# Slot products of a two-layer graph kernel: three buffers of high and low parts, and the next slot's parts ahead of the finished slot's copy

## The chip, the cores and the metric

The kernel runs on one core of a Trainium2 chip. A core has five engines that run side by side and meet only at semaphores: TensorE (PE, matrix products; its weight loads are listed apart as PEld), VectorE (DVE), ScalarE (ACT), GpSimd (POOL) and SyncE (SP, which here issues the DMA transfers). The metric is the device time of one execution in microseconds (us); lower is better.

## The reference, cut to what matters

There are 128 graphs of 128 nodes with 256 features each. Layer 0 is a gated graph convolution with a residual and a layer norm. Layer 1 convolves along the nodes, adds a similarity branch, and mixes both in a gated recurrent cell. The part of interest is the second convolution of layer 1, with 17 taps:

```python
h = _bn(_conv1d(xc, conv1_w, 0), bn1_g, bn1_b, bn1_m, bn1_v)
h = jax.nn.relu(h)
h = _bn(_conv1d(h, conv2_w, 8), bn2_g, bn2_b, bn2_m, bn2_v)
x_conv = jnp.transpose(jax.nn.relu(h + xc), (0, 2, 1))
```

## The kernel before

The kernel is four phases, each ended by a barrier. `phase_a` computes layer 0 and the spectra of the convolution filters (`w_spec` in device memory). `phase_spectrum` computes conv1 and the spectra of its result, which stay on chip in `x_spec`. `phase_product` multiplies the spectra; it is the only phase whose instructions the change alters. `phase_c` transforms back and does the rest of layer 1.

The 17-tap convolution is done as a product of spectra of length 136. Two real rows, a real and an imaginary one, make a slot, so there are 68 slots (`SLOTS`). For a slot s the following is done, once each:

- SP loads the slot's filters, 512 KB, into one of 4 buffers `w` (line 718).
- ACT makes the high part `xh` of the slot's data (line 754) and the high part `wh` of its filters (line 757). DVE makes the low parts by subtraction, `xl` (line 774) and `wl` (line 785).
- PE does 18 matmuls of three passes (low by high, high by low, high by high): 6 with 512 columns and 12 with 256, into one of 4 buffers of `ps` (line 799).
- ACT copies the sums from `ps` to `y` (line 750), and DVE subtracts the product of the imaginary parts (line 781, below called the subtraction).
- SP stores `y`, 256 KB, to `y_spec` (line 729). The first four slots, the rest slots (`REST`), are instead split into `yh` (ACT, line 763) and `yl` (DVE, line 789), and both are stored to `y_rest` (line 726).

Every engine runs the helper `pipeline` over the same step number i. Step i is: SP loads slot i and then stores slot i-3; ACT copies slot i-3 and then makes `xh` and `wh` of slot i-1; DVE makes `xl` of slot i-1, subtracts slot i-3, and makes `wl` of slot i-1; PE multiplies slot i-2. Each engine does its instructions strictly in this order, and each waits for semaphores that count finished slots. The waits that matter here:

- the load of slot i waits until `wl` of slot i-4 is made;
- the store of slot s waits for the subtraction of slot s;
- `xh`, and so `wh` behind it, of slot s waits until PE has finished slot s-2, since there are two buffers of the parts;
- `wh` also waits until its filters have landed; the copy waits until PE has finished its slot;
- the matmuls wait for `xl` and `wl`.

The first 12 steps are written out, the others run in a loop whose body holds 4 steps. Both kernels have this wait of the load and this order on SP:

```python
if live(0):
    reached(sp, s_wl, i - BUFS + 1)
    sp.dma_start(w[:, u]...)
if live(3):
    ...
        reached(sp, s_ys, s)
        sp.dma_start(y_spec[...], y[:, b])
```

Of the kernel before, what the change touches and what calls it, by code (L numbers as in the profile page):

```python
# [7 lines left out]
F32 = mybir.dt.float32  # L8
F32R = mybir.dt.float32r
ALU = mybir.AluOpType  # L10
ACT = mybir.ActivationFunctionType

P = 128
D = 256
KD = D // P
# [7 lines left out]
SLOTS = L // 2  # L23
# [3 lines left out]
CW = 64  # L27
# [3 lines left out]
def reached(eng, sem, count):  # L31

    if isinstance(count, int) and count <= 0:
        return
    eng.wait_ge(sem, count)


def pipeline(eng, units, stages, step, peeled=0, unroll=2):


    first = max(stages, peeled)
    first += -first % unroll
    for i in range(first):
        step(i, i % unroll, i // unroll, lambda s, i=i: 0 <= i - s < units)
    with eng.Fori(first // unroll, units // unroll) as block:
        for u in range(unroll):
            step(block * unroll + u, u, block, lambda s: True)
    for i in range(units, units + stages - 1):
        step(i, i % unroll, i // unroll, lambda s, i=i: 0 <= i - s < units)


# [617 lines left out]
def phase_product(nc, G, x_spec, w_spec, y_spec, y_rest):  # L669


    BUFS = 4
    with ExitStack() as ctx:  # L673
        def sb(name, shape, dt=F32):
            return ctx.enter_context(nc.sbuf_tensor("m_" + name, shape, dt))
# [3 lines left out]


        w = sb("w", [P, BUFS, KD, CHUNKS, 2, CW])
        wh = sb("wh", [P, 2, KD, CHUNKS, 2, CW], F32R)
        wl = sb("wl", [P, 2, KD, CHUNKS, 2, CW], F32R)
        xh = sb("xh", [P, 2, KD, 2, G], F32R)
        xl = sb("xl", [P, 2, KD, 2, G], F32R)
        y = sb("y", [P, BUFS, 2, D])
        yh = sb("yh", [P, 2, 2, D], F32R)
        yl = sb("yl", [P, 2, 2, D], F32R)
# [16 lines left out]
        block = ctx.enter_context(nc.Block())  # L705

        STAGES = 4
        assert SLOTS % BUFS == 0 and REST == BUFS

        def is_rest(s):  # L710
            return isinstance(s, int) and s < REST
# [1 line left out]
        @block.sync  # L713
        def _(sp):
            def step(i, u, k, live):
                if live(0):
                    reached(sp, s_wl, i - BUFS + 1)
                    sp.dma_start(w[:, u].rearrange("p t q r c -> p (t q) (r c)"),
                                 w_spec.rearrange("n p d c -> p n d c")[:, :, bass.ds(2 * i, 2)].rearrange("p n d c -> p n (d c)")
                                 ).then_inc(s_w[u], 16)  # L720
                if live(3):
                    s, b = i - 3, (u - 3) % BUFS
                    if is_rest(s):
                        reached(sp, s_yl, s + 1)
                        for part, rows in enumerate((yh, yl)):
                            sp.dma_start(y_rest[part, 2 * s:2 * s + 2].rearrange("d g c -> g d c"), rows[:, s % 2].bitcast(F32)).then_inc(s_rest[s % 2], 16)
                    else:
                        reached(sp, s_ys, s)
                        sp.dma_start(y_spec[bass.ds(2 * s - 2 * REST, 2)].rearrange("d g c -> g d c"), y[:, b]).then_inc(s_out[b], 16)

            pipeline(sp, SLOTS, STAGES, step, peeled=3 * BUFS, unroll=BUFS)
            for u in range(BUFS):
                sp.wait_ge(s_out[u], 16 * (SLOTS // BUFS - 1))
            for u in range(2):
                sp.wait_ge(s_rest[u], 16 * REST)

        @block.scalar
        def _(act):
            def step(i, u, k, live):
                if live(3):  # L740
                    s, b = i - 3, (u - 3) % BUFS
                    reached(act, s_m, s + 1)
                    if isinstance(s, int) and REST <= s < 2 * REST:

                        act.wait_ge(s_yl, s - REST + 1)
                    if not is_rest(s):

                        at_block = k if b <= u else k - 1
                        reached(act, s_out[b], (at_block - 1) * 16)
                    nc.scalar.activation(y[:, b], ps[:, b, 0], ACT.Copy).then_inc(s_yc, 1)  # L750
                if live(1):
                    s, b, v = i - 1, (u - 1) % BUFS, (u - 1) % 2
                    reached(act, s_m, s - 1)
                    nc.scalar.activation(xh[:, v], x_spec[:, :, bass.ds(s, 1)].rearrange("p c o r g -> p c (o r) g"), ACT.Copy).then_inc(s_xh, 1)
                    at_block = k if b <= u else k - 1
                    reached(act, s_w[b], (at_block + 1) * 16)
                    nc.scalar.activation(wh[:, v], w[:, b], ACT.Copy).then_inc(s_wh, 1)
                if live(3) and is_rest(i - 3):
                    s, b = i - 3, (u - 3) % BUFS
                    reached(act, s_yc, s + 1)  # L760
                    reached(act, s_ys, s)
                    reached(act, s_rest[s % 2], 32 * (s // 2))
                    nc.scalar.activation(yh[:, s % 2], y[:, b], ACT.Copy).then_inc(s_yh, 1)

            pipeline(act, SLOTS, STAGES, step, peeled=3 * BUFS, unroll=BUFS)

        @block.vector
        def _(dve):
            def step(i, u, k, live):
                if live(1):  # L770
                    s, b, v = i - 1, (u - 1) % BUFS, (u - 1) % 2
                    reached(dve, s_xh, s + 1)
                    reached(dve, s_m, s - 1)
                    nc.vector.tensor_tensor(xl[:, v], x_spec[:, :, bass.ds(s, 1)].rearrange("p c o r g -> p c (o r) g"),
                                            xh[:, v].bitcast(F32), ALU.subtract).then_inc(s_xl, 1)
                if live(3):
                    s, b = i - 3, (u - 3) % BUFS

                    if not (isinstance(s, int) and s == 0):
                        reached(dve, s_yc, s + 1)  # L780
                        nc.vector.tensor_tensor(y[:, b, 0], y[:, b, 0], ps[:, b, 1, 0], ALU.subtract).then_inc(s_ys, 1)
                if live(1):
                    s, b, v = i - 1, (u - 1) % BUFS, (u - 1) % 2
                    reached(dve, s_wh, s + 1)
                    nc.vector.tensor_tensor(wl[:, v], w[:, b], wh[:, v].bitcast(F32), ALU.subtract).then_inc(s_wl, 1)
                if live(3) and is_rest(i - 3):
                    s, b = i - 3, (u - 3) % BUFS
                    reached(dve, s_yh, s + 1)
                    nc.vector.tensor_tensor(yl[:, s % 2], y[:, b], yh[:, s % 2].bitcast(F32), ALU.subtract).then_inc(s_yl, 1)

            pipeline(dve, SLOTS, STAGES, step, peeled=3 * BUFS, unroll=BUFS)

        @block.tensor
        def _(pe):
            def three_passes(out, part, v, filters, start, stop):

                for c in range(KD):
                    for t, (xx, ww) in enumerate(((xl, wh), (xh, wl), (xh, wh))):
                        last = nc.tensor.matmul(out.rearrange("p r (q c) -> p r q c", q=CHUNKS), xx[:, v, c, part],  # L799
                                                ww[:, v, c].rearrange("p q r c -> p r q c")[:, filters],  # L800
                                                start=start and c == 0 and t == 0, stop=stop and c == KD - 1 and t == 2)
                return last

            def step(i, u, k, live):
                if live(2):
                    s, b, v = i - 2, (u - 2) % BUFS, u % 2
                    reached(pe, s_xl, s + 1)
                    reached(pe, s_wl, s + 1)
                    reached(pe, s_ys, s - BUFS)
                    reached(pe, s_yc, s - BUFS + 1)  # L810
                    re, im, both = slice(0, 1), slice(1, 2), slice(0, 2)
                    if isinstance(s, int) and s == 0:
                        three_passes(ps[:, b, 0, re], 0, v, re, True, True)
                        three_passes(ps[:, b, 0, im], 1, v, im, True, True).then_inc(s_m, 1)
                    else:
                        three_passes(ps[:, b, 0], 0, v, both, True, False)
                        three_passes(ps[:, b, 0, im], 1, v, re, False, True)
                        three_passes(ps[:, b, 1, re], 1, v, im, True, True).then_inc(s_m, 1)

            pipeline(pe, SLOTS, STAGES, step, peeled=3 * BUFS, unroll=BUFS)  # L820


def phase_c(nc, G, x1_t, y_spec, y_rest, dft_i, bn2, masks, adj_t, w_ih, w_hh, w_msg, w_se, b_ih, b_hh, b_msg, b_se, form, y_n):
# [739 lines left out]
```

## Time and profile before

| | |
|---|---|
| median of 3 runs | 2383.63 us (2381.34 to 2383.7) |
| the profiled execution's own time | 2387.73 us |
| its span, first to last instruction | 2385.9 us |
| mean granted clock of TensorE | 0.949 of full speed |
| busy over the whole span: PE, DVE, ACT, POOL | 88%, 59%, 49%, 30% |
| the product phase | from about 907 to 1151 us, a tenth of the span |

The engines' busy shares are means over four phases that have different limits. What the change is worth must be read inside the product phase, from instructions in order of time.

### The profile page before, as it was taken

The page shows a single profiled execution, that of the slowest core. Times are in us where ns is not written, and L with a number is a line of the kernel's source. Part 1 is how long each engine was busy: PE and PEld are TensorE (multiplying, and loading weights), DVE is VectorE, ACT ScalarE, POOL GpSimd, SP SyncE. Part 2 cuts the span into 40 slices and gives each one's busy share as a digit, 9 for nine tenths or more (in the row PEclk, how much of TensorE's full clock was granted, in tenths as well). Part 3 has the DMA queues.
Part 4 walks back from the last instruction along what each step waited for, and adds up shares of the span by engine and source line. Part 5 has one row for each costly group of instructions (what it writes and reads, how often), then busy time and mean ns, then how long its engine had stood idle before and what let it go on. Part 6 is the DMA issues. An engine that isn't in the chain of part 4 may idle for free.

```text
span 2385.9 us, 37395 instructions
## 1 busy us (share of the span) xinstructions
PE 2090.2 (88%) x12034; PEld 1789.0 (75%) x12034; DVE 1407.4 (59%) x2577; ACT 1180.6 (49%) x1950; POOL 706.5 (30%) x561
## 2 busy tenths in 40 slices
PE   6888788787088886888599999999999999999998
PEld 5777666676078886777478888888888888888886
DVE  5788787798033334666455655656555556565563
ACT  5677666676045555565334444444444444443442
POOL 5667666575600000000012222222222222222222
PEclk9999999898599998999699999999999999999999
DMA  3555455554122215777511211212212122121200
GB/s 119 190 205 199 138 196 201 194 199 172 50 71 70 70 53 172 228 229 230 172 66 51 83 59 65 74 50 82 72 52 82 41 82 74 50 82 50 87 29 27
DMA packets 195906, 263.57 MB, mean 110 GB/s; under 512 B 11914, under 2 KB 141680, under 8 KB 194672
## 3 DMA queue, kind: packets, MB, share of 16 engines
q1 hardware_dynamic: 195824, 262.66, 33.7%
q8 instruction: 29, 0.48, 0.1%
q14 instruction: 53, 0.43, 0.1%
HBM read 174.53 MB, written 88.08 MB: 110 GB/s over the span
## 4 chain that ended last, share of the span: by engine, by line
PE 49%; issue 1%; ACT 1%; DMA 1%; DVE 0%; SPq 0%; POOL 0%; POOLq 0%; ACTq 0%; DVEq 0%
PE c_ps_g L1353 34%; PE c_ps_s L1380 5%; PE c_ps_m L1353 4%; PE c_ps_s L1353 2%; PE c_ps_s L1424 1%; PE c_ps_y L1403 1%; PE c_ps_y L1440 1%; PE c_ps_m L1440 1%; DMA c_yf<-y_spec 1%; PE c_ps_m L1441 0%; PE c_ps_y L1441 0%; ACT c_wi_h L1114 0%; SPq L1005 0%; DVE c_t L1222 0%; SPq L1013 0%
## 5 line engine op out<-in xcount | busy, mean ns | idle before, releaser
L1176 POOL TENSOR_TENSOR c_cl<-c_xc,c_ch 128x512 fp32r<-128x512 f32 x64 | 82.6, 1291 | 488.6 <-ACT c_ch L1068 471.1
L799 PE MATMUL m_ps<-m_wh,m_xl 128*128 128x256 f32 (+1 forms) x406 | 136.9, 337 | 36.8 <-issue 17.2
L1353 PE MATMUL c_ps_g<-c_xh,c_wh_l 128*128 128x512 f32 x384 | 155.6, 405 | 4.2 <-POOL c_cl L1176 4.2
L1252 DVE TENSOR_SCALAR c_work<-c_work 128x512 f32<-128x512 f32 x64 | 27.4, 428 | 219.4 <-ACT c_work L1063 219.4
L1353 PE MATMUL c_ps_g<-c_ch,c_wi_l 128*128 128x512 f32 x384 | 153.6, 400 | 0.0
L1353 PE MATMUL c_ps_g<-c_xl,c_wh_h 128*128 128x512 f32 x384 | 152.4, 397 | 0.0
L1353 PE MATMUL c_ps_g<-c_xh,c_wh_h 128*128 128x512 f32 x384 | 151.9, 396 | 0.0
L1353 PE MATMUL c_ps_g<-c_nh,c_wi_l 128*128 128x512 f32 x384 | 151.7, 395 | 0.0
L1353 PE MATMUL c_ps_g<-c_ch,c_wi_h 128*128 128x512 f32 x384 | 151.7, 395 | 0.0
L1353 PE MATMUL c_ps_g<-c_nh,c_wi_h 128*128 128x512 f32 x384 | 151.7, 395 | 0.0
L1353 PE MATMUL c_ps_g<-c_nl,c_wi_h 128*128 128x512 f32 x384 | 151.6, 395 | 0.0
L1353 PE MATMUL c_ps_g<-c_cl,c_wi_h 128*128 128x512 f32 x384 | 151.5, 394 | 0.0
L1143 POOL MEMSET c_ident<- 128x128 f32 x1 | 0.2, 206 | 502.1 <-POOLq L673 502.1
L1156 POOL TENSOR_TENSOR c_work<-c_xg,c_work 128x512 f32<-128x512 f32 x64 | 89.4, 1397 | 182.9 <-ACT c_work L1058 160.0
L626 DVE SCALAR_TENSOR_TENSOR s_hl<-s_ps_c,s_hh 128x1024 fp32r<-128x1024 f32 x32 | 39.2, 1225 | 165.4 <-ACT s_hh L584 165.4
L799 PE MATMUL m_ps<-m_wl,m_xh 128*128 128x256 f32 (+1 forms) x406 | 130.7, 322 | 0.0
L1068 ACT ACTIVATE c_ch<-c_t,c_shift 128x512 fp32r<-128x512 f32 x64 | 46.3, 724 | 170.0 <-DVE c_t L1222 170.0
L799 PE MATMUL m_ps<-m_wh,m_xh 128*128 128x256 f32 (+1 forms) x406 | 130.3, 321 | 0.0
L799 PEld LDWEIGHTS m_ps<-m_wh,m_xl 128*128 128x128 f32 x406 | 77.9, 192 | 54.3 <-issue 36.2
L432 PE MATMUL a_ps_w<-a_dw,a_gs 102*128 102x272 f32 x256 | 80.2, 313 | 42.2 <-ACT a_spec L242 42.0
L320 POOL TENSOR_TENSOR a_res<-a_ex,a_xn 128x512 f32<-128x512 f32 x64 | 105.8, 1653 | 20.0 <-DMA a_xn<-in_x_n 16.1
L1165 POOL TENSOR_TENSOR c_rstd<-c_var_eps,c_neg_half 128x4 f32<-128x4 f32 x32 | 32.6, 1019 | 265.7 <-DVE c_var_eps L1285 265.7
(220 smaller groups left out, 7300.2 us busy)
## 6 DMA issues: line engine op xcount, KB each, us to landing
w_spec<-a_spec SPq DMA_DIRECT2D x8, 4352.0 KB, 16.8
m_w<-w_spec SPq DMA_DIRECT2D x68, 512.0 KB, 4.0
a_xt<-in_x_t SPq DMA_DIRECT2D x64, 256.0 KB, 3.1
a_xn<-in_x_n SPq DMA_DIRECT2D x64, 256.0 KB, 6.6
x_t<-a_x1t SPq DMA_DIRECT2D x64, 256.0 KB, 2.9
s_x<-x_t SPq DMA_DIRECT2D x32, 512.0 KB, 3.9
y_spec<-m_y SPq DMA_DIRECT2D x64, 256.0 KB, 2.4
c_x<-x_t SPq DMA_DIRECT2D x32, 512.0 KB, 4.1
```

The source lines that it names most:

```text
L320: nc.gpsimd.tensor_tensor(res[:, u], ex[:, :, :], xn[:, u], ALU.add).then_inc(s_res, 1)
L432: nc.tensor.matmul(ps_w[:, 0:GW], gs[:, u, c], dw[:, :], start=True, stop=True).then_inc(s_gm, 1)
L626: nc.vector.scalar_tensor_tensor(hl[:, u], ps_c[:, u], 0.0, hh[:, u].bitcast(F32), ALU.max, ALU.subtract).then_inc(s_hl, 1)
L799: last = nc.tensor.matmul(out.rearrange("p r (q c) -> p r q c", q=CHUNKS), xx[:, v, c, part], ww[:, v, c].rearrange("p q r c -> p r q c")[ ...
L1068: nc.scalar.activation(ch[:, v, j], t2[:, j], ACT.Relu, bias=shift2[:, j:j + 1]).then_inc(s_ch, 1)
L1156: nc.gpsimd.tensor_tensor(dd[:, :], xg[:, v, j], nn[:, :], ALU.subtract).then_inc(s_dd, 1)
L1165: nc.gpsimd.tensor_tensor(rstd[:, :], var_eps[:, :], neg_half[:, :], ALU.pow).then_inc(s_rstd, 1)
L1176: nc.gpsimd.tensor_tensor(cl[:, v, j], xc[:, j], ch[:, v, j].bitcast(F32), ALU.subtract).then_inc(s_cl, 1)
L1252: nc.vector.tensor_scalar(zz[:, :], tz[:, :], 0.5, 0.5, ALU.mult, ALU.add).then_inc(s_zz, 1)
L1353: last = nc.tensor.matmul(out, stationary, moving, start=(n == 0), stop=(n == len(passes) - 1))
L1380: last = nc.tensor.matmul(ps_s[:, b * P:b * P + P], stationary, moving, start=(n == 0), stop=(n == len(passes) - 1))
L1440: nc.tensor.matmul(both, mh[:, b, j * P:j * P + P], ahl[:, b].rearrange("p s n -> p (s n)"), start=True, stop=False)
```

## The change

The parts `wh`, `wl`, `xh`, `xl` get three buffers (`SPLIT`) in place of two, so `xh` of slot s waits for PE to finish slot s-3. On ACT, `xh` and `wh` of slot i-1 now come ahead of the copy of slot i-3. On DVE, `xl` and `wl` of slot i-1 both come ahead of the subtraction of slot i-3. The order on SP and the order on PE stay. The loop body now holds 12 steps, the first 12 steps are written out as before, and the last 11 are written out as well (3 before). The line in `pipeline` changes nothing where the units are a multiple of the unroll, as in the other phases.

```diff
-    for i in range(units, units + stages - 1):
+    for i in range(units - units % unroll, units + stages - 1):
...
+    SPLIT = 3
...
-        wh = sb("wh", [P, 2, KD, CHUNKS, 2, CW], F32R)
-        wl = sb("wl", [P, 2, KD, CHUNKS, 2, CW], F32R)
-        xh = sb("xh", [P, 2, KD, 2, G], F32R)
-        xl = sb("xl", [P, 2, KD, 2, G], F32R)
+        wh = sb("wh", [P, SPLIT, KD, CHUNKS, 2, CW], F32R)
+        wl = sb("wl", [P, SPLIT, KD, CHUNKS, 2, CW], F32R)
+        xh = sb("xh", [P, SPLIT, KD, 2, G], F32R)
+        xl = sb("xl", [P, SPLIT, KD, 2, G], F32R)
...
+        UNROLL = BUFS * SPLIT
+        assert REST == BUFS
+
+        def turns(k, u, back):
+
+            return k * SPLIT + (u - back) // BUFS
...
             def step(i, u, k, live):
+                if live(1):
+                    s, b, v = i - 1, (u - 1) % BUFS, (u - 1) % SPLIT
+                    reached(act, s_m, s - SPLIT + 1)
+                    nc.scalar.activation(xh[:, v], x_spec[:, :, bass.ds(s, 1)].rearrange("p c o r g -> p c (o r) g"), ACT.Copy).then_inc(s_xh, 1)
+                    reached(act, s_w[b], (turns(k, u, 1) + 1) * 16)
+                    nc.scalar.activation(wh[:, v], w[:, b], ACT.Copy).then_inc(s_wh, 1)
                 if live(3):
                     s, b = i - 3, (u - 3) % BUFS
                     reached(act, s_m, s + 1)
...
                     nc.scalar.activation(y[:, b], ps[:, b, 0], ACT.Copy).then_inc(s_yc, 1)
-                if live(1):
-                    s, b, v = i - 1, (u - 1) % BUFS, (u - 1) % 2
-                    reached(act, s_m, s - 1)
-                    nc.scalar.activation(xh[:, v], x_spec[:, :, bass.ds(s, 1)].rearrange("p c o r g -> p c (o r) g"), ACT.Copy).then_inc(s_xh, 1)
-                    at_block = k if b <= u else k - 1
-                    reached(act, s_w[b], (at_block + 1) * 16)
-                    nc.scalar.activation(wh[:, v], w[:, b], ACT.Copy).then_inc(s_wh, 1)
...
                 if live(1):
-                    s, b, v = i - 1, (u - 1) % BUFS, (u - 1) % 2
+                    s, b, v = i - 1, (u - 1) % BUFS, (u - 1) % SPLIT
                     reached(dve, s_xh, s + 1)
-                    reached(dve, s_m, s - 1)
+                    reached(dve, s_m, s - SPLIT + 1)
                     nc.vector.tensor_tensor(xl[:, v], x_spec[:, :, bass.ds(s, 1)].rearrange("p c o r g -> p c (o r) g"),
                                             xh[:, v].bitcast(F32), ALU.subtract).then_inc(s_xl, 1)
+                    reached(dve, s_wh, s + 1)
+                    nc.vector.tensor_tensor(wl[:, v], w[:, b], wh[:, v].bitcast(F32), ALU.subtract).then_inc(s_wl, 1)
                 if live(3):
                     s, b = i - 3, (u - 3) % BUFS
 
                     if not (isinstance(s, int) and s == 0):
                         reached(dve, s_yc, s + 1)
                         nc.vector.tensor_tensor(y[:, b, 0], y[:, b, 0], ps[:, b, 1, 0], ALU.subtract).then_inc(s_ys, 1)
-                if live(1):
-                    s, b, v = i - 1, (u - 1) % BUFS, (u - 1) % 2
-                    reached(dve, s_wh, s + 1)
-                    nc.vector.tensor_tensor(wl[:, v], w[:, b], wh[:, v].bitcast(F32), ALU.subtract).then_inc(s_wl, 1)
...
-            pipeline(dve, SLOTS, STAGES, step, peeled=3 * BUFS, unroll=BUFS)
+            pipeline(dve, SLOTS, STAGES, step, unroll=UNROLL)
...
-                    s, b, v = i - 2, (u - 2) % BUFS, u % 2
+                    s, b, v = i - 2, (u - 2) % BUFS, (u - 2) % SPLIT
```

## Rows read from the trace of the kernel before

**Rows 1.** Waits, product phase (us in total, times, longest); the last from SP's queue.

```profile
ACT m_y L750 <- PE m_ps L799: 89.0, 65, 3.6
...
ACT m_wh L757 <- DMA m_w<-w_spec: 11.0, 8, 3.5
...
SPq L729 <- DVE m_y L781: 140.7, 63, 4.9
```

**Rows 2.** Timeline of ACT: start us, duration us, instruction [idle before].

```profile
1040.98 0.60 ACT L750 ACTIVATE m_y<-m_ps 128x512 f32<-128x512 f32 x1 [1.66 <-PE m_ps L799]
1041.47 0.62 ACT L754 ACTIVATE m_xh<-x_spec 128x512 fp32r x1
1041.99 1.05 ACT L757 ACTIVATE m_wh<-m_w 128x1024 fp32r<-128x1024 f32 x1
...
1047.78 0.60 ACT L750 ACTIVATE m_y<-m_ps 128x512 f32<-128x512 f32 x1 [1.65 <-PE m_ps L799]
```

**Rows 3.** Timeline of DVE, the same steps.

```profile
1042.24 0.69 DVE L774 TENSOR_TENSOR m_xl<-x_spec,m_xh 128x512 fp32r<-128x512 f32 x1 [1.57 <-ACT m_xh L754]
1042.85 0.41 DVE L781 TENSOR_TENSOR m_y<-m_y,m_ps 128x256 f32<-128x256 f32 x1
1043.18 1.22 DVE L785 TENSOR_TENSOR m_wl<-m_w,m_wh 128x1024 fp32r<-128x1024 f32 x1
```

**Rows 4.** Timeline of PE: first matmul of a slot behind a stall, and of two in a row.

```profile
941.01 0.77 PE L799 MATMUL m_ps<-m_wh,m_xl 128*128 128x512 f32 x1 [2.52 <-issue]
...
1044.59 0.49 PE L799 MATMUL m_ps<-m_wh,m_xl 128*128 128x512 f32 x1 [0.65 <-issue]
...
1047.81 0.49 PE L799 MATMUL m_ps<-m_wh,m_xl 128*128 128x512 f32 x1 [0.15 <-issue]
```

**Rows 5.** SP's queue: loads of slots 12 and 67; between, two stores and loads.

```profile
951.22 0.40 SPq L718 DMA_DIRECT2D m_w<-w_spec  x1
...
1043.44 0.38 SPq L729 DMA_DIRECT2D y_spec<-m_y  x1
1044.02 0.39 SPq L718 DMA_DIRECT2D m_w<-w_spec  x1
1046.52 0.38 SPq L729 DMA_DIRECT2D y_spec<-m_y  x1
1047.43 0.39 SPq L718 DMA_DIRECT2D m_w<-w_spec  x1
...
1139.49 0.39 SPq L718 DMA_DIRECT2D m_w<-w_spec  x1
```

**Rows 6.** Landing times of the 68 filter loads and 8 stores of filters.

```profile
DMA to landing us min/median/max: 3.8/4.0/17.6
```

**Rows 7.** Timeline of ACT, DVE and SP's queue while the rest slots are stored.

```profile
924.87 1.06 ACT L757 ACTIVATE m_wh<-m_w 128x1024 fp32r<-128x1024 f32 x1 [1.37 <-DMA m_w<-w_spec]
...
925.96 1.23 DVE L785 TENSOR_TENSOR m_wl<-m_w,m_wh 128x1024 fp32r<-128x1024 f32 x1 [1.40 <-ACT m_wh L757]
...
927.11 0.69 DVE L789 TENSOR_TENSOR m_yl<-m_y,m_yh 128x512 fp32r<-128x512 f32 x1
...
927.82 0.37 SPq L726 DMA_DIRECT2D y_rest<-m_yh  x1
...
928.75 0.50 SPq L718 DMA_DIRECT2D m_w<-w_spec  x1
...
933.02 1.06 ACT L757 ACTIVATE m_wh<-m_w 128x1024 fp32r<-128x1024 f32 x1 [1.52 <-DMA m_w<-w_spec]
```

**Rows 8.** Timeline, the one place in the loop where filters were late.

```profile
967.18 1.06 ACT L757 ACTIVATE m_wh<-m_w 128x1024 fp32r<-128x1024 f32 x1 [0.32 <-DMA m_w<-w_spec]
...
968.28 1.23 DVE L785 TENSOR_TENSOR m_wl<-m_w,m_wh 128x1024 fp32r<-128x1024 f32 x1
```

**Rows 9.** Stretches: length, busy PE, PEld, DVE, ACT, POOL, clock, DMA share, GB/s.

```profile
942.00:944.00 2.00, 2.00 (x7) 1.63 (x6) 1.13 (x1) 0.00 (x0) 0.00 (x0) 0.50 0.55 162
954.00:1142.00 188.00, 167.56 (x991) 143.80 (x990) 119.33 (x168) 113.87 (x166) 0.00 (x0) 1.00 0.79 230
```

More of the change, by code:

```diff
@@ L707, in phase_product @@
         STAGES = 4
-        assert SLOTS % BUFS == 0 and REST == BUFS
+        UNROLL = BUFS * SPLIT
+        assert REST == BUFS
+        def turns(k, u, back):
+            return k * SPLIT + (u - back) // BUFS
         def is_rest(s):
@@ L717, in step @@
                     reached(sp, s_wl, i - BUFS + 1)
-                    sp.dma_start(w[:, u].rearrange("p t q r c -> p (t q) (r c)"),
+                    sp.dma_start(w[:, u % BUFS].rearrange("p t q r c -> p (t q) (r c)"),
                                  w_spec.rearrange("n p d c -> p n d c")[:, :, bass.ds(2 * i, 2)].rearrange("p n d c -> p n (d c)")
-                                 ).then_inc(s_w[u], 16)
+                                 ).then_inc(s_w[u % BUFS], 16)
                 if live(3):
@@ L729, in step @@
                         sp.dma_start(y_spec[bass.ds(2 * s - 2 * REST, 2)].rearrange("d g c -> g d c"), y[:, b]).then_inc(s_out[b], 16)
-            pipeline(sp, SLOTS, STAGES, step, peeled=3 * BUFS, unroll=BUFS)
+            pipeline(sp, SLOTS, STAGES, step, unroll=UNROLL)
             for u in range(BUFS):
@@ L746, in step @@
                     if not is_rest(s):
-                        at_block = k if b <= u else k - 1
-                        reached(act, s_out[b], (at_block - 1) * 16)
+                        reached(act, s_out[b], (turns(k, u, 3) - 1) * 16)
                     nc.scalar.activation(y[:, b], ps[:, b, 0], ACT.Copy).then_inc(s_yc, 1)
-                if live(1):
-                    s, b, v = i - 1, (u - 1) % BUFS, (u - 1) % 2
-                    reached(act, s_m, s - 1)
-                    nc.scalar.activation(xh[:, v], x_spec[:, :, bass.ds(s, 1)].rearrange("p c o r g -> p c (o r) g"), ACT.Copy).then_inc(s_xh, 1)
-                    at_block = k if b <= u else k - 1
-                    reached(act, s_w[b], (at_block + 1) * 16)
-                    nc.scalar.activation(wh[:, v], w[:, b], ACT.Copy).then_inc(s_wh, 1)
                 if live(3) and is_rest(i - 3):
@@ L763, in step @@
                     nc.scalar.activation(yh[:, s % 2], y[:, b], ACT.Copy).then_inc(s_yh, 1)
-            pipeline(act, SLOTS, STAGES, step, peeled=3 * BUFS, unroll=BUFS)
+            pipeline(act, SLOTS, STAGES, step, unroll=UNROLL)
         @block.vector
@@ L818, in step @@
                         three_passes(ps[:, b, 1, re], 1, v, im, True, True).then_inc(s_m, 1)
-            pipeline(pe, SLOTS, STAGES, step, peeled=3 * BUFS, unroll=BUFS)
+            pipeline(pe, SLOTS, STAGES, step, unroll=UNROLL)
 def phase_c(nc, G, x1_t, y_spec, y_rest, dft_i, bn2, masks, adj_t, w_ih, w_hh, w_msg, w_se, b_ih, b_hh, b_msg, b_se, form, y_n):
```

## The prediction

> **What bounds the phase now.** The change touches only the product phase, so the whole-kernel shares decide nothing, and three of the four phases keep their instructions. I read four views of the phase: the waits, the timeline of each engine around 1040 us, SP's queue, and the stretches.
>
> The waits say that ACT stood 89.0 us for PE before its copies, and only 11.0 us for filters, 8 times; and that SP stood 140.7 us for the subtraction before its stores [rows 1]. The first names today's limit. The last looks harmless, yet SP issues in order and the next load stands behind that store.
>
> Pace: the loop issues the loads of slots 12 to 67 from 951.22 to 1139.49 us, 55 intervals in 188.27 us, so 3.423 us a slot [rows 5]. PE alone would be faster: between two first matmuls lie 3.22 us with 0.15 us of idle, so some 3.07 us of work [rows 4]. What holds it at 3.42 is a circle over two slots. PE finishes slot 35 and ACT starts its copy (1040.98), then `xh` of slot 37 (+0.49), then `wh` (+0.52); DVE starts `wl` 1.19 us later, behind its subtraction; `wl` takes 1.22; PE starts slot 37 0.19 us after (1044.59) and ACT copies it at 1047.78, 3.19 us on. Sum: 0.49+0.52+1.19+1.22+0.19+3.19 = 6.80 us for two slots, 3.40 each [rows 2, 3, 4], which is the pace. (Slot numbers: load 12 is at 951.22, so the one at 1044.02 is number 39, the store before it 35.)
>
> **What the change removes.** With three buffers `xh` and `wh` of slot 37 need PE's slot 34, not 35, and stand ahead of the copy of slot 35. The circle above is cut; if nothing else held it, PE's 3.07 us would be the pace.
>
> **What the change closes.** Three orders stay or are new: the load of slot n+2 is issued behind the store of slot n-2 (SP, as before); that store waits for the subtraction of slot n-2; and this subtraction now stands behind `wl` of slot n on DVE, and its copy behind `wh` of slot n on ACT. But `wh` of slot n needs the load of slot n. So load n leads to `wh` n, `wl` n, subtraction n-2, store n-2, load n+2: a circle over two slots with a whole DMA transfer in it. Before, subtraction n-2 stood ahead of `wl` n and the copy ahead of `wh` n, so the same walk went through `wh` of slot n-1 and spanned three slots: with the numbers below, 3.95 landing, 0.97 to 0.99 `wh`, 0.49 copy, 0.77 `xh` to `xl` start, 0.61 to the subtraction's start [rows 2, 3], 0.41, 0.18, 0.65 = about 8.0 us for three, 2.7 each. Filters were on time, by 0.8 us: slot 39's load went out at 1044.02 and landed near 1048.0, its `wh` came 1.01 us behind the copy of 1047.78, at 1048.79 [rows 2, 5].
>
> The length of the new circle, term by term:
>
> - `wh` on ACT 1.05 us [rows 2], and 0.04 us to the start of `wl` where DVE waits for it: 967.18+1.06 = 968.24, `wl` at 968.28 [rows 8].
> - `wl`: the next DVE instruction starts 1.15 us behind its start (925.96 to 927.11) [rows 7], the pipelined form of its 1.22. I take 1.14. By then the copy, begun about 0.97 us after `wh`'s start, is over, so it adds nothing.
> - The subtraction 0.41; then 0.18 us to the store's issue: 1042.85+0.41 = 1043.26, issue at 1043.44 [rows 3, 5].
> - Store to load on SP: 0.58 and 0.91 us in two cases [rows 5]. The larger is the one of four steps that takes in the loop's turn; with 12 steps in the body it comes once in 12. I take 0.65.
> - Load issue to landing: median 4.0, least 3.8 [rows 6]; where ACT waited for it, `wh` started 933.02-928.75 = 4.27 us after issue in the written-out part [rows 7], whose issue itself is 0.1 us longer. I take 3.95, by the loop's median.
>
> Sum: 1.05+0.04+1.14+0.41+0.18+0.65+3.95 = 7.42 us for two slots, 3.71 a slot. That is longer than PE's 3.07 and than today's 3.42.
>
> The trace holds a test of this walk. While the rest slots are stored, `yl` stands behind `wl` in just that way: `wh` 924.87, `wl` 925.96, `yl` 927.11 (0.69), store 927.82, load 928.75, next-but-one `wh` 933.02. The whole turn is 8.15 us, and it waited for the DMA at both ends [rows 7]. The new circle has 0.41 for 0.69 and one store for two. So every link has been seen; new is that it runs for the whole loop.
>
> **The sum.** 55 intervals by (3.71-3.42) = +15.8 us. After the last load the path was: landing, 0.8 us of waiting for the copy, `wh`, `wl`, PE, copy, subtraction, store. The waiting goes, the rest is equal: -0.8 us. The written-out start: `wh` of slot 2 no longer waits for PE's slot 0, which brings the first stores up to 2 us forward; but in the four rest slots subtraction, `yh` and `yl` now all stand behind `wl`: `yh` (0.6 us) and the subtraction (0.41) join the 8.15 us turn, about +0.5 us a slot, +2 us. I take zero and keep 2 us either way. The added 8 written-out steps at the end change a link by 0.2 us or so and go into the range. Memory for the third buffers costs no time; the instructions are as many as before. PE's 0.3 to 0.4 us saved a slot lie beside the circle and are worth nothing.
>
> Total +15.0 us: 2387.73 becomes about 2402.7 for a profiled execution, which was 4.1 us above the median of the runs; on the median, 2383.63+15.0 = 2398.6 us, +0.63%. Bounds of the circle: landing 3.8 and 0.58 between store and load give 7.20 (3.60 a slot, +9.7-0.8 = +9); landing 4.27 and the mean of today's two issue gaps, 0.75, give 7.84 (3.92, +27.3-0.8 = +26.5). With the start's 2 us: 2391 to 2412.
>
> **Rivals.**
>
> 1. Faster, because loads return sooner than I think. The circle without its landing is 3.47 us; it equals today's two slots (6.85) at a landing of 3.38 us, and leaves the lead to PE (6.14) at 2.67. With PE leading, 55 by -0.35 = -19.4, and -0.8: about 2363; a landing half way gives 2373. For it: the engines of the DMA are 0.79 busy in the loop [rows 9], and slower steps would leave them emptier. Against it: the shortest landing of all is 3.8 us [rows 6]. Chance 0.10. The Trainium skill, "DMA: Bandwidth & Descriptors", section "Anatomy of one DMA", fits a transfer as 2.0 us plus bytes over 436 GB/s, for a path issued by GpSimd; by it 512 KB would land in an estimated 3.2 us, the circle would be 3.34 a slot, and the kernel would come out at 2378 us. The trace disagrees, with 3.8 us as its least, for SP's queue.
> 2. No change that can be told (within 0.2%, a bound of about what a measurement of this kernel can tell): the links in the loop overlap more than I add up, the circle is 6.7 to 7.0 us, +-4 us in all. For it: each of seven links could be 0.1 us short. Against it: the turn of 8.15 us shows nearly the same links at full length, one behind the other. Chance 0.08.
> 3. Slower by more: transfers of odd and even slots drift together and delay one another, so landings go from 4 to 4.5 us or more: 8.0 a turn, +32 us, 2415. For it: a DMA share of 0.79. Against it: store and load of a circle keep their distance, and the longer step lowers the share to about 0.73. Chance 0.06.
> 4. PE's clock. PE gets idle gaps of 0.6 us a slot on average and unequal ones may reach 1.5. Behind a stall of 2.52 us [rows 4] the clock was at the lower of its levels, 0.50 (1.2 GHz), at 942 to 944 us [rows 9]; in the loop it stands at 1.00. A single fall is hidden, since a slot's copy is needed more than 2 us after PE ends it. If it stayed low, a slot would take about 6.1 us on PE: +140 us. Chance 0.03, with the loop's longer code among what could disturb it.
>
> **Numbers.** Forecast 0.73; rivals 0.10, 0.08, 0.06, 0.03. The likeliest gives 2398.6 us. The range 2386 to 2418 reaches into rival 2 below and takes in rival 3; it leaves out rival 1, rival 4 and half of rival 2. Faster by over 0.2%: 0.10. Within: 0.08. Slower by over 0.2% (above 2388.4): 0.82.
>
> **What will show it.** In the changed kernel, nearly every `wh` of the loop should be preceded by idle time that a DMA of filters ended (some 60 times, of 0.8 us or more each, for 11.0 us before), the waits for PE before the copies should be gone from ACT, `wl` should start 0.04 us behind `wh`, the subtraction should start 1.14 us behind `wl`, and every second `wh` start should be 7.2 to 7.8 us apart. PE should wait for `wl`, and DMA share should fall to about 0.73. The prediction is wrong if landings come in well below 3.8 us, if SP's loads aren't held by the subtraction, or if the phase's own start or end moves by more than 3 us.

## The result, and the profile after

The changed kernel takes 2396.1 us (median of 4 runs, 2393.52 to 2398.76) against 2383.66 us before; the ratio is 1.0054, with a 95% interval of 1.0036 to 1.0071. It is slower by 12.4 us. The forecast was slower by 15.0, at 2398.6 us.

First the waits of the product phase after the change (who waited for whom: us in total, times, longest).

```profile
ACT m_wh L752 <- DMA m_w<-w_spec: 104.2, 65, 3.3
DVE m_wl L782 <- ACT m_wh L752: 99.3, 66, 3.6
...
ACT m_y L762 <- PE m_ps L802: 4.6, 3, 3.5
```

ACT's wait for PE before its copies has gone from 89.0 us to 4.6, as the change says it should. In its place ACT waits for filters 65 times in 68 slots, 104.2 us against 11.0 [rows 1], and DVE's `wl` waits for that `wh`. SP's own queue waits for the subtraction even longer than before, 161.6 us:

```profile
SPq L736 <- DVE m_y L788: 161.6, 63, 4.0
```

Next the timeline of ACT (start us, duration us), one turn of the circle and the `wh` in between.

```profile
1040.07 1.06 ACT L752 ACTIVATE m_wh<-m_w 128x1024 fp32r<-128x1024 f32 x1 [1.70 <-DMA m_w<-w_spec]
1041.03 0.58 ACT L762 ACTIVATE m_y<-m_ps 128x512 f32<-128x512 f32 x1
...
1043.52 1.06 ACT L752 ACTIVATE m_wh<-m_w 128x1024 fp32r<-128x1024 f32 x1 [1.39 <-DMA m_w<-w_spec]
...
1047.35 1.06 ACT L752 ACTIVATE m_wh<-m_w 128x1024 fp32r<-128x1024 f32 x1 [1.76 <-DMA m_w<-w_spec]
```

DVE in the same turn:

```profile
1041.16 1.23 DVE L782 TENSOR_TENSOR m_wl<-m_w,m_wh 128x1024 fp32r<-128x1024 f32 x1 [1.61 <-ACT m_wh L752]
1042.30 0.41 DVE L788 TENSOR_TENSOR m_y<-m_y,m_ps 128x256 f32<-128x256 f32 x1
```

and SP's queue in the same turn:

```profile
1042.89 0.38 SPq L736 DMA_DIRECT2D y_spec<-m_y  x1
1043.47 0.39 SPq L725 DMA_DIRECT2D m_w<-w_spec  x1
```

Read together, these are the predicted links in the predicted order: `wh` at 1040.07, ending 1041.13; `wl` 0.03 us later; the subtraction 1.14 us behind `wl`'s start; 0.18 us from its end (1042.71) to the store's issue; 0.58 us to the load's issue; 3.88 us to the next-but-one `wh` at 1047.35. The sum is 1.06+0.03+1.14+0.41+0.18+0.58+3.88 = 7.28 us. Over the stretch 960 to 1090 us two slots take 7.35 us on average. The early turns are the longer ones: 7.46 us on average over slots 12 to 28, 7.26 from there to slot 67.

PE waits before each slot (first matmuls of two slots in a row), where before it had stood 0.65 and 0.15 us [rows 4]:

```profile
1042.58 0.49 PE L802 MATMUL m_ps<-m_wh,m_xl 128*128 128x512 f32 x1 [0.69 <-issue]
1045.94 0.47 PE L802 MATMUL m_ps<-m_wh,m_xl 128*128 128x512 f32 x1 [0.30 <-issue]
```

SP's queue again, the loads of slots 12 and 67, and the stretch of the loop (length, busy PE, PEld, DVE, ACT, POOL, clock, DMA share, GB/s):

```profile
943.65 0.40 SPq L725 DMA_DIRECT2D m_w<-w_spec  x1
...
1144.82 0.47 SPq L725 DMA_DIRECT2D m_w<-w_spec  x1
```

```profile
954.00:1142.00 188.00, 157.35 (x926) 134.95 (x927) 110.98 (x155) 105.47 (x154) 0.00 (x0) 1.00 0.73 215
```

55 intervals in 201.17 us are 3.658 us a slot, against 3.423 [rows 5]: 55 by 0.235 = +12.9 us. The DMA share fell from 0.79 [rows 9] to 0.73, as forecast, and the clock stayed at 1.00. The whole phase, from the first filter load to the end of the last store's issue, took 256.1 us against 244.6, +11.5. The two profiled spans differ by 6.2 us only (2392.1 and 2385.9), mostly because the phases ahead of the product, which have the same instructions in both, ended 6.7 us earlier in this execution: the first filter load was issued at 899.9 us here and at 906.5 before, and between 898 and 908 us in all the profiles below. So the pace of the phase is read inside it, and whole times are compared over several runs.

### The profile page after: what moved, and what is told of

It is laid out like the page before. It is cut to its first block, busy times and chain, and to the rows that moved or that the text cites. A ratio compares the mean times of both kernels' runs of the same rounds, so it can differ in the third digit from the quotient of the medians.

```text
span 2392.1 us, 37206 instructions
## 1 busy us (share of the span) xinstructions
PE 2083.9 (87%) x12034; PEld 1783.3 (75%) x12034; DVE 1407.0 (59%) x2577; ACT 1180.2 (49%) x1950; POOL 706.4 (30%) x561
## 4 chain that ended last, share of the span: by engine, by line
PE 49%; issue 1%; ACT 1%; DMA 0%; DVE 0%; SPq 0%; POOL 0%; POOLq 0%; ACTq 0%; DVEq 0%
PE c_ps_g L1356 34%; PE c_ps_s L1383 5%; PE c_ps_m L1356 4%; PE c_ps_s L1356 2%; PE c_ps_s L1427 1%; PE c_ps_y L1406 1%; PE c_ps_y L1443 1%; PE c_ps_m L1443 1%; DMA c_yf<-y_spec 0%; PE c_ps_m L1444 0%; PE c_ps_y L1444 0%; ACT c_wi_h L1117 0%; SPq L1008 0%; SPq L1016 0%; DVE c_t L1225 0%
## 5 line engine op out<-in xcount | busy, mean ns | idle before, releaser
L782 DVE TENSOR_TENSOR m_wl<-m_w,m_wh 128x1024 fp32r<-128x1024 f32 x68 | 83.3, 1225 | 99.4 <-ACT m_wh L752 99.3
L752 ACT ACTIVATE m_wh<-m_w 128x1024 fp32r<-128x1024 f32 x68 | 72.1, 1060 | 104.3 <-DMA m_w<-w_spec 104.2
```

## The experiments

Each run was timed in turn with the kernel before on the same chip, and its ratio is to those times. "Pace" is the time a slot takes in the loop, from the loads of slots 12 and 67, or, where marked *, from the copies between 1000 and 1080 us.

| run | edit | time, us | ratio to before (95%) | pace, us |
|---|---|---|---|---|
| before | | 2381.4 to 2384.1 (medians) | | 3.423 |
| changed | | 2396.1 | 1.0054 (1.0036 to 1.0071) | 3.658 |
| E1 | changed, stores a step later | 2343.33 | 0.9822 (0.9806 to 0.9839) | 2.854 |
| E2 | changed, DVE's old order | 2385.76 | 1.0001 (0.9989 to 1.0014) | 3.408 |
| E3 | changed, both old orders | 2380.05 | 0.9988 (0.9973 to 1.0003) | 3.360 |
| E4 | changed, two buffers | 2401.17 | 1.0066 (1.0049 to 1.0082) | 3.730 |
| E5 | before, stores a step later | 2376.69 | 0.9981 (0.9970 to 0.9993) | 3.418 |
| E6 | changed, half loads | 2369.43 | 0.9954 (0.9938 to 0.9970) | 3.229 |
| E7 | changed, stores on GpSimd's queue | 2339.77 | 0.9833 (0.9802 to 0.9864) | 2.82* |
| E8 | E4, stores a step later | 2362.6 | 0.9917 (0.9893 to 0.9941) | 3.101 |
| E9 | E3, stores a step later | 2371.51 | 0.9955 (0.9942 to 0.9968) | 3.322 |
| E10 | before, DVE's new order | 2406.43 | 1.0088 (1.0064 to 1.0113) | 3.767 |

### E1: the load freed from the store

```diff
-                if live(3):
-                    s, b = i - 3, (u - 3) % BUFS
+                if live(4):
+                    s, b = i - 4, (u - 4) % BUFS
...
-            pipeline(sp, SLOTS, STAGES, step, unroll=UNROLL)
+            pipeline(sp, SLOTS, 5, step, unroll=UNROLL)
```

> The changed kernel with one edit on SP alone: the store of slot s is issued one step later, so the load of slot n+2 stands behind the store of slot n-3 and no longer behind that of n-2. Theory (circle through the load): the same links of 7.3 us now span three slots, 2.45 a slot, so the circle lets go. What is left is PE with 3.07 us a slot (3.0 to 3.15): 55 by -0.35 us against the kernel before, so 2361 to 2368 us; ACT's waits for filters nearly vanish. Rival A (the transfers themselves are the bound, since they take 0.73 to 0.79 of the DMA engines): the pace stays at 3.6 us or more, 2394 or above. Rival B (third buffers or the longer loop are the cost): no change from the changed kernel's 2396.

Measured: 2343.33 us, 53 us below the changed kernel and 40 below the kernel before. The direction is the theory's, the size is not: it said 2361 to 2368. Rivals A and B are out: the same bytes, buffers and loop went through in 2.854 us a slot. The stretch of E1's loop, then, between 960 and 1090 us, ACT's wait for the loads (us, times) and their landing times:

```profile
940.00:1080.00 140.00, 138.71 (x873) 124.69 (x872) 105.59 (x148) 102.52 (x148) 0.00 (x0) 1.00 0.92 274
```

```profile
  ACT m_wh L752: 31.2, 37
...
DMA to landing us min/median/max: 3.9/5.2/6.7
```

PE is busy 138.71 of 140 us, so it leads, but at 2.85 us a slot and not at 3.07. One sign that was expected failed: ACT's waits for filters did not nearly vanish. 37 of the 46 `wh` in this stretch still waited for their load, 31.2 us in all. The loads now take 5.2 us to land (median), at a DMA share of 0.92, and with that landing the circle's links come to 1.06+0.03+1.14+0.41+0.18+0.58+5.2 = 8.6 us for three slots, an estimated 2.87 a slot. So the circle is spread over three slots but hardly slack: it is as long as the pace that was measured, within 0.02 us. It holds PE up little, for E7, where no `wh` waits for a load, is only 0.03 us a slot faster.

### E2: only DVE's order undone

```diff
                 if live(1):
...
                     nc.vector.tensor_tensor(xl[:, v], ...
-                    reached(dve, s_wh, s + 1)
-                    nc.vector.tensor_tensor(wl[:, v], ...
                 if live(3):
...
                         nc.vector.tensor_tensor(y[:, b, 0], ...
+                if live(1):
+                    reached(dve, s_wh, s + 1)
+                    nc.vector.tensor_tensor(wl[:, v], ...
```

> The changed kernel with DVE's order as before: the subtraction of slot n-2 ahead of wl of slot n; ACT keeps the new order, three buffers stay. Theory: the circle stays over two slots, but runs from wh past the copy (0.97 to its start, 0.58, 0.05 to DVE) in place of past wl (1.06, 0.03, 1.14): 0.97+0.58+0.05+0.41+0.18+0.58+3.88 = 6.65 us, 3.33 a slot against 3.66; about 55 by -0.33 = -18 us from the changed kernel, 2376 to 2383 us. Rival (ACT's order or the buffers or the loop's length set the pace, not DVE's order): stays within 4 us of 2396.

Measured: 2385.76 us, 3.408 us a slot. The rival is out, 10 us (13 by the ratios) went with DVE's order alone; the time is 3 us above the theory's range. ACT, DVE and SP's queue of this run show where:

```profile
1042.15 1.06 ACT L752 ACTIVATE m_wh<-m_w 128x1024 fp32r<-128x1024 f32 x1 [1.57 <-DMA m_w<-w_spec]
1043.12 0.58 ACT L762 ACTIVATE m_y<-m_ps 128x512 f32<-128x512 f32 x1
...
1043.73 0.42 DVE L786 TENSOR_TENSOR m_y<-m_y,m_ps 128x256 f32<-128x256 f32 x1 [1.49 <-ACT m_y L762]
...
1044.91 0.39 SPq L725 DMA_DIRECT2D m_w<-w_spec  x1
```

`wh` to load is 2.76 us, as laid out (2.77), and `wh` is still released by the DMA (44 times between 960 and 1110 us): the circle runs through the copy now. With the median landing of 4.0 us of this run in place of 3.88 it is 6.8 us; two slots took 6.88 on average. So both orders, not DVE's alone, put a late link into the circle.

### E3: the buffers and the loop without the orders

The edit takes E2's and puts ACT's copy ahead of `xh` and `wh` again.

> Three buffers and the 12-step loop, but both orders, ACT's and DVE's, as before. Theory: xh of slot n stands behind the copy of slot n-2 on ACT whatever its semaphore says, so the old circle of 6.80 us over two slots through PE is what remains: 3.40 to 3.42 a slot, 2380 to 2387 us, the kernel before. Rival (the third buffers alone free PE): 3.07 a slot, 2364. Rival (buffers or loop length are the cost of the change): 2390 or above.

Measured: 2380.05 us, a ratio whose interval holds 1, at 3.36 us a slot. Third buffer and 12-step loop cost nothing, and bring 0.06 us a slot at most, while `xh` stands behind the copy in ACT's queue. That order alone holds `xh`, whatever the buffer count; with the order changed, two buffers hold it too, though less (E8).

### E4: the orders without the third buffer

```diff
-    SPLIT = 3
+    SPLIT = 2
```

and 16 steps written out ahead of a loop of 8.

> The changed kernel's orders with two buffers of the parts (16 steps written out ahead, a loop of 8). Theory: the circle through the load does not use the third buffer; xh of slot n must now wait for PE's slot n-2, which ends about 5.5 us after that slot's wh began and so 1 us before xh is needed: still 3.66 a slot, 2392 to 2400 us. Rival (the third buffer is what moves the time, either way): below 2388 or above 2404.

Measured: 2401.17 us, inside neither the 2392 to 2400 of the theory nor the 2404 of the rival. ACT still waits for filters (lines of the waits, product phase):

```profile
ACT m_wh L752 <- DMA m_w<-w_spec: 70.1, 60, 3.2
...
ACT m_xh L750 <- PE m_ps L802: 31.9, 53, 2.5
```

`xh` is held by PE 53 times and yet `wh` behind it waits for the DMA 60 times, so the circle through the load leads with two buffers as well. It is 0.07 us a slot slower than the changed kernel (4 us over the loop) and takes 47.4 us to the load of slot 12 against 43.8. The 4 us are spread: two slots take 7.66, 7.42 and 7.35 us on average over slots 12 to 28, 28 to 44 and 44 to 67, where the changed kernel takes 7.46, 7.27 and 7.25. In the written-out start the granted clock of this profile was 0.72 at 910 to 920 us, 0.73 at 930 to 935 and 0.70 at 940 to 945, and `xh` waited for PE there up to 2.5 us; the changed kernel's clock was 1.00 from 910 us on. How much of the 3.6 us of the start is the clock's and how much the missing buffer's, no run splits off, and the rest of the loop's 4 us isn't settled either.

### E5: the later stores without the change

The same edit as E1, made in the kernel before.

> The kernel before (two buffers, old orders) with the stores issued one step later. Theory: before, the load's circle spans three slots and is slack, and the pace is the circle of 6.80 us over two slots through PE, copy, xh, wh, wl; moving the stores cannot touch it: 3.42 a slot in the loop, and at most a few us from the written-out start, 2375 to 2386 us. Rival (the later store alone is worth most of the 40 us that it brought on top of the changed kernel): 2350 or below.

Measured: 2376.69 us and 3.418 us a slot. The loop does not move. The 5 us come from outside it: the load of slot 12 is issued 35.1 us after the first load, against 44.7 before, but from the load of slot 67 to the end of the last store's issue it is 14.8 us against 11.6, so that the phase is 6.7 us shorter in this profile, and not 9.6. The later store is worth its 53 us only where the load's circle leads.

### E6: a shorter transfer

From slot 4 on this kernel loads only the first of the two halves (KD) of each filter tile and multiplies old values for the other, so it leaves out half of the filters.

```diff
+                    parts = KD * CHUNKS if isinstance(i, int) and i < BUFS else CHUNKS
-                    sp.dma_start(w[:, u % BUFS].rearrange("p t q r c -> p (t q) (r c)"),
-                                 w_spec.rearrange("n p d c -> p n d c")[:, :, ...
+                    sp.dma_start(w[:, u % BUFS].rearrange("p t q r c -> p (t q) (r c)")[:, 0:parts],
+                                 w_spec.rearrange("n p d c -> p n d c")[:, 0:parts, ...
```

> The changed kernel with only half of each filter load, 256 KB for 512, from slot 4 on (the other half of the buffer keeps old filters); everything else is issued the same. Theory: what the transfer gets shorter leaves the circle in full: a landing of 3.88 should become about 2.9 (the stores, of the same bytes in larger packets, land in 2.4), so 7.3 - 1.0 = 6.3 a turn, 3.15 a slot, 55 by -0.5 = -28 us from the changed kernel, 2360 to 2376. Rival (the pace is set by links on ACT and DVE alone, the transfer beside them): within 4 us of 2396.

Measured: 2369.43 us, in the theory's range, 27 us below the changed kernel. The loads' landing times (whole phase) and the waits between 960 and 1110 us:

```profile
DMA to landing us min/median/max: 2.8/3.0/17.0
```

```profile
ACT m_wh L753 <- DMA m_w<-w_spec: 53.9, 39, 2.4
```

The landing fell by 0.9 us, and so did two slots of the loop: 2 by (3.658-3.229) = 0.86 us. What a transfer on a circle gets shorter, the circle gives back in full.

### E7: the stores on another queue

The block of the stores moves from SP to GpSimd's queue, in the same step and behind the same waits; SP issues loads only.

```diff
+        @block.gpsimd
+        def _(pool):
+            def step(i, u, k, live):
+                if live(3):
...
+                        reached(pool, s_ys, s)
+                        pool.dma_start(y_spec[...], y[:, b]).then_inc(s_out[b], 16)
```

> The changed kernel with the stores, all of them, issued by GpSimd's queue in the same step instead of SP's; SP issues loads alone. Theory: nothing about bytes or waits changes but that no load stands behind a store any more, so the circle is open and PE leads as in the run with the later stores: 2.85 to 3.0 a slot, 2340 to 2358 us, if GpSimd issues a store in less than a slot. Rival (the gain of the later stores came from their timing against the loads on the DMA engines, not from the order in the queue): stays near 2396.

Measured: 2339.77 us, at the lower end of what the theory said. Nothing but the stores' queue differs in the program from the changed kernel. The waits (960 to 1110 us), and the stretch of its loop:

```profile
ACT m_y L768 <- PE m_ps L808: 41.4, 51, 2.2
```

```profile
940.00:1080.00 140.00, 140.00 (x895) 127.19 (x894) 116.31 (x150) 102.34 (x151) 36.16 (x50) 1.00 0.91 280
```

No `wh` waits for filters any more, ACT waits for PE again, and PE is busy for the whole stretch. This answers what E1 left open: it was the load's place behind the store in one queue. The rival, a better meeting of stores and loads on the DMA engines, would have to show in the landings, and they got longer: 5.4 us (median, 960 to 1090 us) against 3.9.

### E8: what the third buffer is worth

> The changed kernel's orders with two buffers and the later stores. Theory: the load's circle is slack, and with two buffers xh of slot n waits for the end of PE's slot n-2: 0.15+0.52+1.09+1.22+0.2 and 2.9 on PE = 6.1 us over two slots, 3.05 a slot: 55 by -0.37 = -20 and some 8 for the shorter start, 2352 to 2362 us. That would show what the third buffer is worth once the loads are free. Rival (the third buffer is worth nothing): 2343, as with three.

Measured: 2362.6 us, 0.6 us above the theory's 2352 to 2362; 3.10 us a slot against 3.05. The waits between 960 and 1110 us name PE before `xh`:

```profile
ACT m_xh L750 <- PE m_ps L802: 51.3, 49, 1.5
```

With the stores a step later, the third buffer is worth 19 us (2362.6 to 2343.3), or 23 by the two ratios, 0.9917 and 0.9822. With the loads on the circle it was covered.

### E9: old orders, three buffers, stores later

> Three buffers, the old orders on ACT and DVE, and the stores one step later. Theory: with xh of slot n behind the copy of slot n-2 in ACT's queue, the old circle through PE of 6.8 us over two slots holds whatever the buffers and the stores do: 3.36 to 3.42 a slot, 2368 to 2380 us, as the kernel before with the later stores (2377). So the 40 us of the best runs need the new order too. Rival (with loads free, three buffers are enough): below 2360.

Measured: 2371.51 us, 3.322 us a slot. The old circle holds, a little below the range given for its pace. It is 0.10 us a slot faster than E5, which has two buffers and the four-step loop: PE's first matmul starts on average 1.36 us behind the start of `wl` here and 1.46 there (960 to 1110 us). Which of buffers and loop does it, no run separates. So E1's whole gain takes three things together: buffers, orders and later stores. Orders and later stores without the third buffer (E8) bring half of it, and each of the other two pairs (E9, the changed kernel) less or a loss.

### E10: the smallest edit that makes the loss

The kernel before with `wl` and the subtraction exchanged on DVE, two buffers, nothing else.

> The kernel before with one pair of DVE instructions exchanged and nothing else: wl of slot n ahead of the subtraction of slot n-2. Theory: this alone closes the circle through the load, wh 1.06, 0.03, wl 1.14, subtraction 0.41, 0.18, store to load 0.70 (the loop of four steps), landing 3.9 = 7.4 us over two slots, 3.7 a slot, 55 by +0.28 = +15 us: 2392 to 2402, with ACT's wh released by the DMA nearly every time. Rival (ACT's order or the third buffer is the harmful part): 2378 to 2386, as before.

Measured: 2406.43 us, 4 us above the range, 22 above the kernel before; the rival is out. The four steps of this loop have four gaps between store and load: 0.92 us across the loop's turn, then 0.65, 0.64 and 0.58. Every second load belongs to the same circle, so there are two circles, and one of them always has the 0.92:

```profile
1038.55 0.38 SPq L729 DMA_DIRECT2D y_spec<-m_y  x1
1039.19 0.39 SPq L718 DMA_DIRECT2D m_w<-w_spec  x1
...
1045.97 0.38 SPq L729 DMA_DIRECT2D y_spec<-m_y  x1
1046.89 0.39 SPq L718 DMA_DIRECT2D m_w<-w_spec  x1
```

With the gaps 0.92 and 0.64 and landings of 3.96 its turns are 7.70 and 7.42 us, 7.56 on average; the other's, with 0.58 and 0.65 (loads at 1042.39 and 1049.83), are 7.36 and 7.43. The slower one sets the pace: the loop measured 7.53, where 7.4 was laid out: 55 by (3.767-3.423) = +18.9 us. The written-out start adds 2.3 us (47.0 us to the load of slot 12, against 44.7).

One fall of the clock adds to this. Between 975 and 978 us the granted clock was 0.54, and ACT's copy, which in this kernel still stands ahead of `xh` and `wh`, had to wait for that slot:

```profile
978.44 0.60 ACT L750 ACTIVATE m_y<-m_ps 128x512 f32<-128x512 f32 x1 [3.34 <-PE m_ps L799]
```

The `wh` behind it (979.46) did not wait for its load, issued 4.51 us before at 974.95, and the turn took 7.91 us in place of 7.36.

## Why the prediction was right, point by point

- **What bounds the phase before**, the circle over two slots through PE, copy, `xh`, `wh` and `wl`: right. E3 and E9 keep it with more buffers, E5 with later stores; it stays between 3.32 and 3.42 us a slot in all of them.
- **What the change removes**: right in the waits (89.0 to 4.6 us of ACT on PE). E8 and E1 show that both the order and the buffers are needed for it.
- **What the change closes**: right, link by link. E1 spreads the circle over a third slot, E7 opens it, E6 shortens it, E10 makes it by itself in the kernel before.
- **The sum**: +15.8 us was forecast for the loop and +12.9 came. The circle was laid out at 7.42 us and measured at 7.28 in the turn shown and 7.32 by the pace. The term that was too large is above all the landing, 3.95 against 3.88 in the turn shown. Store to load was taken as 0.65; it was 0.58 in most steps, but 0.92 across the turn of the 12-step loop and 0.65 and 0.64 in the two steps behind it, so 0.65 on average over the circle that has the turn, 0.59 over the other, and 0.62 over both. The two terms make up the 0.10 us a turn. The end was put at -0.8 and gave -0.5; the written-out start was put at 0 and gave -0.9 (43.8 us to the load of slot 12, against 44.7). In all +11.5 in the phase, +12.4 in the medians. The start is compared at unequal clocks: before, the granted clock was 0.66 at 910 to 920 us and again at 940 to 945 us, and after it was 1.00 in both, so how much of the -0.9 is the change's isn't shown.
- **PE's own pace** was mis-sized, and with it rival 1's price. I took 3.07 us a slot from two starts 3.22 us apart less the 0.15 us of idle shown [rows 4]. A slot whose operands lie ready takes 2.82 to 2.85 us (E7, E1). The rows of E7 show where the 0.25 us went, at the border of two slots with no wait:

```profile
1047.60 0.28 PE L808 MATMUL m_ps<-m_wh,m_xh 128*128 128x256 f32 x1
1047.72 0.40 PE L808 MATMUL m_ps<-m_wh,m_xl 128*128 128x512 f32 x1
1047.95 0.40 PE L808 MATMUL m_ps<-m_wl,m_xh 128*128 128x512 f32 x1
```

  The last matmul is listed with 0.28 us, yet the next slot's first starts 0.12 behind it, and the second 0.23 behind the first. Before, the last matmul started at 1047.38 and the next slot's first at 1047.81, 0.43 behind it: the idle of 0.15 counts from the end of the listed 0.28, so the gap was 0.31 longer than in E7. The second matmul then started 0.33 behind the first (1048.14), 0.10 more. That is 0.16 and 0.10 us that the row's idle time leaves out. The forecast did not use the 3.07, but it made the chance missed look like 20 us where it was 40.
- **Rival 1** (faster by early landings) failed as argued: the shortest landing was 3.7 us after the change. **Rival 2** (a circle of 6.7 to 7.0 us by overlap) failed: its links came at full length. **Rival 3** (landings that grow): landings of 5.2 and 5.4 us do come at DMA shares of 0.92 and 0.91 (E1, E7), but 3.9 us is what E8 still shows at 0.87, and the longer step had lowered the share to 0.73. **Rival 4**: the clock held 1.00 over the loop with idle of 0.3 to 0.8 us a slot. By its own numbers its price was 55 by (6.1-3.42) = +147 us and not +140. Its remark that a single fall of the clock is hidden was not tested in the changed kernel; in E10, with the old order on ACT, one fall cost its turn 0.55 us.

The fastest kernels found, E7 and E1, are 56 and 53 us below the changed one: the change was sound on ACT and DVE and needed the stores out of the loads' way.

## What to carry to other kernels

Before making an instruction earlier in an in-order queue, list what it now stands ahead of, and follow that to its end: here a subtraction, behind it a store, behind that in SP's queue a load, and the load fed the very instruction that was moved. Count over how many units such a walk returns to itself; the same links that were slack over three slots led over two. And if a profile shows a DMA queue waiting long for a store's data, ask what loads are issued behind it.

## What the runs showed that I had not expected

- A 512 KB load lands in 3.9 us (median) at a DMA share of 0.73 and still at 0.87 (E8), but in 5.2 us at 0.92 (E1) and 5.4 at 0.91 (E7), all from SP's queue. In E7 no `wh` waited for the slower landings.
- Half of that load lands 0.9 us sooner (3.9 to 3.0), so the second 256 KB cost 0.9 us, about 290 GB/s. The Trainium skill, "DMA: Bandwidth & Descriptors", section "Anatomy of one DMA", puts the part that grows with size at bytes over 436 GB/s for transfers that GpSimd issues, an estimated 0.6 us for the same bytes; these transfers, from SP's queue, took half as long again.
- PE's first matmul behind a late operand cost more than the idle time that the row shows: 3.07 us a slot by that reading, 2.82 without any wait. The difference lies in the last matmul's listed duration, which overlaps the next one when nothing waits, and in a slower first matmul.
- The issue gap from a store to the next load on SP was 0.58 us in most steps of the long loop, but 0.92 across its turn and 0.65 and 0.64 in the two steps behind it. With a loop of four steps one of the two circles paid 0.92 and 0.64 in turn: 7.56 us on average in E10, for 7.36 with 0.58 in every step.
